# More DMA completion lanes in a two-stage kernel: 12 to 16 on the SyncE queue, 6 to 8 on the GpSimd queue

## The reference

```python
# attention block
xn = layernorm(x) * gamma + beta
v, x1, x2 = split(xn @ W_in + b_in, 3)          # W_in: 1024 x 3072
y = causal_conv(v, k0) * x1                     # per channel, 128 taps
y = causal_conv(y, k1) * x2
a = x + y @ W_out + b_out
x = layernorm(x + a)
# ffn block (weights w1: 4096 x 1024, w2: 1024 x 4096, rounded to -1, 0, 1 times a scale)
h = quant(rmsnorm(x)) @ wq(w1).T                # quant: to 8 bit with a scale per row
h = act_scale * relu(h)**2 + act_bias
y = quant(rmsnorm(h)) @ wq(w2).T
x = layernorm(x + y)
```

## Time and profile before

| | before |
|---|---|
| time, median of 2 runs | 3087.43 us (3086.51 to 3088.34) |
| the profiled execution, device time | 3093.75 us |
| its span on the slowest core (core 3) | 3092.2 us |
| spans of the other cores | 3069.0 to 3089.5 us |
| DVE busy | 1600.4 us, 52% of the span |
| TensorE busy | 1412.2 us, 46% |
| ACT busy | 787.5 us, 25% |
| DMA queue of SP, share of the 16 DMA engines | 10.6% |
| DMA queue of POOL | 8.6% |

### The profile page before, as it was taken

The page is one execution under the profiler, slowest core; times in us unless marked ns, Lnnn a source line. Parts: engine busy times, 40 slices in busy tenths (PEclk is TensorE's granted clock), DMA queues, the critical chain, the costliest instruction groups (busy, mean ns, idle before and its releaser), DMA issues.

```text
span 3092.2 us, 19657 instructions; the slowest of 8 cores (3069.0 to 3092.2 us)
## 1 busy us (share of the span) xinstructions
PE 1412.2 (46%) x4270; PEld 444.3 (14%) x4270; DVE 1600.4 (52%) x1675; ACT 787.5 (25%) x1164; POOL 71.2 (2%) x128
## 2 busy tenths in 40 slices
PE   2676676666656610000024455544444554444453
PEld 0122121222212100000001111111111111111110
DVE  3223334343343434556025667776666676666665
ACT  0010111111111000000004444444444444444442
POOL 0000000000000011101000000000000000000000
PEclk9876677777877755555557666666667766667675
DMA  3400000000000046678930000101100110001001
GB/s 87 163 14 0 11 21 11 16 16 11 21 11 14 7 126 184 224 253 290 171 66 13 24 20 24 27 21 24 25 24 20 25 24 25 24 24 24 20 22 28
DMA packets 203438, 166.45 MB, mean 54 GB/s; under 512 B 173625, under 2 KB 178490, under 8 KB 199227
## 3 DMA queue, kind: packets, MB, share of 16 engines
q1 hardware_dynamic: 186716, 82.34, 10.6%
q0 software_dynamic: 16608, 82.85, 8.6%
HBM read 100.09 MB, written 29.36 MB: 42 GB/s over the span
## 4 chain that ended last, share of the span: by engine, by line
DVE 43%; issue 13%; PEldq 12%; DMA 11%; SPq 9%; ACT 7%; PEld 3%; DVEq 2%; ACTq 1%; POOLq 0%
DVE g2s L889 14%; PEldq L175 11%; DMA wqf<-w 7%; DVE Pb L663 5%; SPq L1017 5%; ACT d2s L882 3%; DVE f2s L879 3%; DVE xq2o L895 3%; DVE d2s L892 2%; DVE wqb L811 1%; SPq L844 1%; SPq L837 1%; DVEq L175 1%; DVE st_mu L517 1%; DVE wsum L776 1%
## 5 line engine op out<-in xcount | busy, mean ns | idle before, releaser
L987 PE MATMUL pj<-wq1T,xq1T 128*128 128x512 bf16 x1024 | 399.5, 535 | 646.0 <-ACTq L175 332.7
L889 DVE SCALAR_TENSOR_TENSOR g2s<-d2s,g2s 128x1024 bf16<-128x1024 bf16 x352 | 431.2, 1225 | 42.9 <-issue 1.4
L1026 PE MATMUL yc<-wq2T,xq2Tc 128*128 128x512 bf16 x1024 | 296.6, 427 | 138.8 <-DMA xq2Tc<-xq2o 123.6
L987 PEld LDWEIGHTS pj<-wq1T,xq1T 128*128 128x128 bf16 x1024 | 115.6, 122 | 934.8 <-issue 907.6
L882 ACT ACTIVATE d2s<-f2s 128x1024 bf16<-128x1024 bf16 x64 | 67.7, 1057 | 363.9 <-DVEq L175 363.9
L1026 PEld LDWEIGHTS yc<-wq2T,xq2Tc 128*128 128x128 bf16 x1024 | 105.1, 104 | 326.4 <-issue 255.4
L941 ACT ACTIVATE t<-xp 128x1024 f32<-128x1024 bf16 x16 | 16.9, 1058 | 528.1 <-PEq L175 473.6
L605 PE MATMUL yc<-Wg,xnT 128*128 128x512 bf16 x576 | 145.1, 398 | 2.9
L605 PE MATMUL pj<-Wg,xnT 128*128 128x512 bf16 x288 | 111.2, 556 | 72.9 <-DVEq L175 72.9
L672 PE MATMUL pj<-Pb,s_winv 128*128 128x512 bf16 x198 | 99.1, 568 | 80.7 <-DVEq L175 80.7
L522 ACT ACTIVATE st_mu<-st_mu 128x1 f32<-128x1 f32 x34 | 6.9, 203 | 497.9 <-DVEq L175 497.9
(11 more groups left out here) (181 smaller groups left out, 2067.6 us busy)
## 6 DMA issues: line engine op xcount, KB each, us to landing
wqf<-w POOLq DMA_DIRECT2D x64, 512.0 KB, 3.9
wqf<-w POOLq DMA_DIRECT2D x16, 2048.0 KB, 12.0
wf<-W_in SPq DMA_DIRECT2D x8, 1536.0 KB, 8.7
xr<-x_own POOLq DMA_DIRECT2D x16, 512.0 KB, 4.3
sc_wq<-wqb SPq DMA_DIRECT2D x32, 256.0 KB, 2.1
sc_wq<-wqb SPq DMA_DIRECT2D x8, 1024.0 KB, 5.0
xq2Tc<-xq2o SPq DMA_TRANSPOSE x512, 2.3
out<-outb SPq DMA_DIRECT2D x16, 512.0 KB, 2.8
```

The lines of the kernel that those rows point to most:

```text
L889: tn = sch.op("vector", (lambda lv: lambda e: e.scalar_tensor_tensor(gbuf[:, 0:width], dbuf[:, 0:width], 0.5 + lv, gbuf[:, 0:width], OP.is ...
L987: (lambda ss, dc, h: lambda e: e.matmul(pshalf("pj", h), xq1T[:, dc * 128:(dc + 1) * 128], wq1T[dc][:, ss * 1024 + h * 512: ss * 1024 + (h ...
L1026: (lambda k, q, oc, kb: lambda e: e.matmul(pshalf("yc1", oc), xq2Tc[kb][:, q * 128:(q + 1) * 128], wq2Tc[k * 8 + q][:, oc * 512:(oc + 1) * ...
```

## The change

One line: the kinds of lanes become 16 and 8. The list of semaphores, the lane of every DMA, its wait for the earlier DMA on the lane, all tokens and `sch.barrier()` follow from it. No operation is added, removed or moved, and no buffer changes.

```diff
-_DMA_LANES = {"DS": 12, "DQ": 6}
+_DMA_LANES = {"DS": 16, "DQ": 8}
 _SEMS = (("T", "V", "S", "Q")
          + tuple(f"DS{i}" for i in range(_DMA_LANES["DS"]))
          + tuple(f"DQ{i}" for i in range(_DMA_LANES["DQ"])))
```

## The result

| | before | after |
|---|---|---|
| median of the runs, us | 3090.41 (3085.37 to 3115.43, 42 runs) | 3098.06 (3091.93 to 3110.91, 43 runs) |
| profiled execution, us | 3093.75 | 3105.17 |
| its span (slowest core), us | 3092.2 | 3103.6 |

The ratio after to before is 1.0024, with a 95% interval of 1.0017 to 1.0030. That is +7.4 us (5.3 to 9.3). More lanes made the kernel slower by a quarter of a per cent. The forecast was +4.4, in the range and with the right sign, but somewhat too small.

A forecast was written before the change was run, and what follows sets the result against it. The prediction took SP to be held by the DMA issue itself, not by lanes. Its terms, 3.85 + 0.70 - 0.10 - 0.05 = +4.4 us, on a median of 3087.4 gave 3091.8 us, range 3083 to 3101.

The forecast's parts named there:

- (a): SP's lane wait, 12 back to 16 back: already satisfied at once, gain 0; four first-use waits fewer, gain under 0.1 us.
- point (1): Sign in the profile after: SP's waits again without one for a lane, issues again 1.24 us apart.
- (b): POOL's start: loads go out about 3 to 4 us sooner; effect taken as 0, bounds -2.4 and +6.9 us.
- point (2): Sign at POOL's start: last x load issued at about 14 to 15 us, not 18.04; three table-load landings within 1 us.
- rival 2: POOL's earlier loads slow SP's table loads at the start: +6.9 us, giving 3098.7; chance 0.07.
- (c): Number of waits elsewhere: five more before ACT's cast in `emit_stageF`, 0.055 us each, in tiles 2 to 15: +3.85 us.
- (d): The barriers: 14 more satisfied waits on SP at `barrierW`, +0.70 us; `barrierA` on POOL 0; final wait -0.10.
- point (4): Sign at `barrierW`: 24 wait pieces before L837, taking 1.2 us instead of 0.5.
- Rival 1: The extra waits are absorbed or hidden by the runs' own spread: 3087; chance 0.16.
- point (5): Sign in the profile after: one iteration 0.27 us longer than the present one.
- rival 3: ACT's longer wait row stalls 0.52 us once a tile: +7.3, 3099.1; chance 0.04 below the 2% line, 0.01 above.

## Why the prediction was right, and where it was too small

**SP is not bound by lanes, (a) and point (1): right.** No wait for a lane, the issue as long as before, and the run with SP's lanes alone is slower, not faster. Eight waits of SP fall away and not four, four of them behind `barrierW`, about 0.2 us.

**POOL's start, (b) and point (2): right in the sum.** The last x load goes out at 15.48 us (14 to 15 had been forecast), and the matrices are ready at the same time. Table for table the three landings stay within the margin of 1 us: 8.7 for 8.84, 7.51 for 7.12, 4.34 for 4.66. The run with POOL's lanes alone gives 1.0005, at most 1.0015, and rival 2's 6.9 us would be 1.0022: rival 2 is out. The rule of the Trainium skill weighed there (DMA: Bandwidth & Descriptors, "Queues, rings and completion order") had given 0, and the runs agree within that interval.

**The number of waits, (c): right in count, place and price.** Eight pieces in `emit_stageF`, and idle times before the casts of the four chunks as forecast. Timeline of ACT in one iteration, after, chunks 0 to 3 (forecast 0.54, 0.1, 0.49, 0.54):

```profile
2219.26 1.15 ACT L876 ACTIVATE it2s<-t2f,st_m 128x1024 int32<-128x1024 f32 x1 [0.54 <-issue]
...
2224.26 1.15 ACT L876 ACTIVATE it2s<-t2f,st_m 128x1024 int32<-128x1024 f32 x1
...
2241.88 1.15 ACT L876 ACTIVATE it2s<-t2f,st_m 128x1024 int32<-128x1024 f32 x1 [0.49 <-issue]
...
2256.86 1.15 ACT L876 ACTIVATE it2s<-t2f,st_m 128x1024 int32<-128x1024 f32 x1 [0.54 <-issue]
```

Moving these waits away, seven and not five, gave back 6.7 of the 7.5 us, and 40 added ones cost 0.055 each, 0.050 by the times. The Trainium skill (Advanced Engine Details and Errata, "Network/Comms") gives 50 to 100 ns for the reading of a semaphore by a sequencer, and these lie at its lower end. Its upper end would have come to an estimated +7.6 for the whole sum, near the measured +7.4, but for a wrong reason, since no wait cost 0.1.

**The barriers, (d) and point (4): right**, 24 pieces and 1.2 us. Rival 1 is out, as the interval of the ratio leaves 1 out.

**The iteration, point (5): too small.** +0.27 us was forecast, +0.54 measured. The step that fell short is not one of the terms but what (c) left out: it let an extra instruction cost something only where it stands, and put the change of all that comes behind it at nothing. Over the stage, 14 tiles:

| term | us |
|---|---|
| five waits before the cast, 14 x 0.275 (forecast) | 3.85 |
| ACT's pauses at that cast, 14 x 0.046 (0.321 measured, less 0.275) | 0.65 |
| DVE's pauses, 14 x 0.110 | 1.5 |
| SP's long issues on the stretch up to L938, 14 x 0.152 | 2.1 |
| the other stretches, 14 x -0.040 | about -0.6 |
| sum; measured 7.5 | 7.5 |

DVE's 0.110 a tile was reproduced by one instruction (0.124), and 0.10 of SP's 0.152 by ten on PE. The remaining 0.05 of SP's was not reproduced. ACT's 0.046 was not tested alone; it is the pauses in tiles 2 and 7, of which the chain above shows the second. No run has the one on DVE and the ten on PE together at 12 lanes, so that their effects add up is taken and not shown. In sum: +7.5 in the stage and +0.7 at `barrierW`, 8.2, within the 5.3 to 9.3 of the times.

The time itself, 3098.06 us, is 6.3 above the 3091.8 of the forecast. About half of that, 3.0, is the base, since the median of two runs had been 3087.43 and that of 42 is 3090.41; only the rest is the pauses. That the 3098.7 of rival 2 and the 3099.1 of rival 3 lie nearer is chance: what they describe isn't in the traces.

Rival 3 came near to it, by a misread row. It took the 0.52 us of the earlier trace rows for a stall in a row of waits and priced it at once a tile. But that piece isn't one: in front of POOL's single loads L566 and L773, which stand behind one wait or two, there are 0.50 us as well. The pauses of the other sequencers, 0.3 to 0.5 us, come with the place in the stream, not with the row of waits. They fall in front of something important only now and then, and what decides it is any instruction ahead of them. The prediction counted DVE's and PE's waits within an iteration, where they don't change, and the three of PE on tile 0, and not those ahead of the stage, of which DVE has one more and PE seven.

## What to carry to other kernels

Raising the number of semaphores on which DMAs are handed out saves nothing if no trace row waits for one. It can add instructions elsewhere, since each consumer waits for each lane. Count the waits of the engine that is on the path, and where a later operation has already waited for all of them, wait for that one instead. If a small difference is to be explained to the last microsecond, look also at what shifts in every sequencer's stream. For a large gain look at the order in the queue first: a load that stood behind transposes it doesn't need cost 4.1 us a tile here, and five waits cost 0.27.

## What the runs showed of the hardware

- A satisfied wait costs its queue 0.055 us on ACT (0.050 by the times of 560 of them), and 0.05 on SP (23 of them in 1.14 us at `barrierW`).
- ACT's, SP's and DVE's sequencers pause for about 0.35 us (0.40 to 0.46 on DVE) at places that lie multiples of 128 instructions apart, waits included, and behind such a place the trace has an instruction packet of 8192 bytes (503 of 576 places before, against 3 of 576 halfway between them). PE's instruction packets have 16384 bytes, 39 for 9971 records.
- A pause that falls on the increment behind a running operation costs nothing; the same one in front of an operation costs 0.40 us on DVE. One more instruction at the start of the kernel decides between the two: +0.23 us a tile in the run with one more on DVE, 0.12 of it in the four DVE stretches.
- The issue of a DMA transpose on SP takes 1.16 to 1.19 us, and over 1.4 and up to 2.6 in 130 of 5120 cases, each of which meets an instruction packet, 122 of them one of PE's. Ten more instructions on PE moved these places; changes to the streams of SP, DVE or ACT did not. How the fetch holds up the issue stays open.
